# Key-length floor by a pairwise maximum on VectorE, and the division by the denominators on ScalarE, in the context attention of a decoder kernel

## The chip, the cores and the metric

The kernel runs on one core of a Trainium2 chip. A core has five engines that run their own instruction streams and meet at semaphores: TensorE (PE in the profile, with its weight loads as a row of their own, PEld), VectorE (DVE), ScalarE (ACT), GpSimd (POOL) and SyncE (SP), which only issues DMAs here. SBUF is the working memory and PSUM takes what TensorE writes. The metric is the device time of one execution in microseconds (us), as the median of several runs. Three runs of the kernel before gave 1176.01, 1176.21 and 1176.6 us.

## The reference, cut to what matters

The whole program is a two-layer decoder over x of shape (32, 56, 128): a state-space mixer, an attention over a context, a mixture of experts, and then the same three kinds once more, with a layer norm after each. Only the first layer's context attention is touched. Its inputs are the context (32, 1500, 128) with a mask, and x as 56 latents per batch. It has two heads of 64.

```
def rmsnorm(x, gamma):
    n = jnp.linalg.norm(x, axis=-1, keepdims=True) * x.shape[-1] ** (-0.5)
    return x / jnp.maximum(n, RMS_EPS) * gamma            # RMS_EPS = 1e-08
xn = layernorm(x, ln_x_g, ln_x_b)                         # x: the context here
ln = layernorm(latents, ln_l_g, ln_l_b)
q = ln @ W_q
kv = jnp.concatenate([xn @ W_kv, ln @ W_kv], axis=1)
...
qn = rmsnorm(q, q_gamma) * SCALE
kn = rmsnorm(k, k_gamma)
sim = jnp.einsum('bhid,bhjd->bhij', qn, kn)
sim = jnp.where(full_mask[:, None, None, :], sim, neg)
attn = jax.nn.softmax(sim, axis=-1)
out = jnp.einsum('bhij,bhjd->bhid', attn, v)
return out.transpose(0, 2, 1, 3).reshape(b, nl, INNER) @ W_out + b_out
```

## The kernel before

The stage in question is `stage_context` (lines 1184 to 1536). It treats the 32 batches one after the other in a pipeline. One batch's context of 1500 positions lies in SBUF as 125 partitions by 12 tiles of 128 features. The key matrix and the queries are folded together before the stage, so that a batch needs these products on TensorE: 12 transposes of the normalised context (`turn`, L1466), 12 products that give the keys whose lengths are needed (`keys`, L1483), 12 products that give raw scores with 12 for the mask before them (`scores`, L1494 and L1490), one transpose and one product that spread each column's maximum to all partitions (`turn_peaks` L1511, `widen_peaks` L1515), 12 products that mix the context by the probabilities (`mix`, L1531) and two that make the output rows with their denominators (`values`, L1522 and L1523). Data are f32, and each f32 product or weight load is two records in the trace.

Every engine runs the same loop: the function `steps` goes through 38 iterations k, and in each it calls the parts of that engine's list in the order written, a part with lag j working on batch k - j. This order is written by hand and is the whole schedule; each engine takes its instructions strictly in this order, with waits on semaphores.

- VectorE, in one iteration: `statistics` (12 bn_stats of batch k, L1302), `overall` (maximum of the transposed column maxima, L1341), `scale` (three multiplications of raw scores by the inverse key lengths, out of PSUM, L1314), `weigh` (batch k - 6), `maximum` (column maxima of the scores, L1334), `lengths` (batch k - 2). `weigh` waits for the output rows in PSUM, takes the reciprocal of the two denominators (L1322), waits for it, and multiplies the rows of each head by it (two instructions of 56 x 64, L1326) into `att`. `lengths` sums the squares of the keys in three reduces of 512 to 8 elements (L1348), waits for the third, and applies the floor 1e-16 * 64 to the 24 sums in place by a tensor_scalar (L1352).
- ScalarE: `evict_two` and `evict_last` (transposed context out of PSUM, L1364), `take_mix` (L1380), `inverse` (Ln and Exp of the floored sums, L1387 and L1389), `diagonal` (L1412), `exponential` (L1402 and L1405), `take_latents` (L1397), `square_two` and `square_last` (squares of the keys out of PSUM, L1426), `take_peak` (L1419), `normalise` (2 of the 12 tiles, L1439), `roots` (L1448, L1451). Their order is in the statement that ends the ScalarE block.
- GpSimd: `subtract` (the maxima from all 1456 scores of each partition, one long tensor_tensor, L1256), `normalise` (10 of the 12 tiles, L1266 to L1271), `moments` (six small operations, L1282 to L1290). At the start it fills eight buffers (L1251) and counts them in the semaphore `const`.
- SyncE loads a batch's context (750 KB) when its buffer is free (L1241).

TensorE's `mix` and `values` both write the PSUM bank `pO`, and both wait for `att` of the batch before, so the division must have read the rows of one batch before the next mix starts.

Of the kernel before, what the change touches and what calls it, by code (L numbers as in the profile page):

```python
# [16 lines left out]
ALU = mybir.AluOpType  # L17
# [7 lines left out]
P = 128  # L25
# [11 lines left out]
KP = 125  # L37
# [1146 lines left out]
def stage_context(core, sb, psum, mk, mv_ext, qw, latS, vl, att, bout, negmask, onehot, xc, ctx_loads):  # L1184
# [15 lines left out]
    shift = sb("shift", [KP, 2, KT])  # L1200
    xcT = sb("xcT", [D, 2, KT * KP])
    sq = sb("sq", [KP, 2, KS, HB, DH])
    ss = sb("ss", [KP, 2, KT, HB])
    inv = sb("inv", [KP, 2, KT, HB])
    sc = sb("sc", [P, 3, KT + 1, QR])
    top = sb("top", [P, 2, QR])
    topall = sb("topall", [P, 2, QR])
    plat = sb("plat", [P, QP])
    mixT = sb("mixT", [D, 2, QP])
    rden = sb("rden", [P, HB])  # L1210
    peak = sb("peak", [QR, 2])
    diag = sb("diag", [QR, 2, QR])
    pX = psum("pX", [P, SUB, 512])
# [6 lines left out]
             "top topT peak diag wide topall subbed probs mix mixT val rden att").split()  # L1220
    s = {n: core.sem(f"bl_{n}") for n in names}
    HALF = D // 2

    def context(n):
        return xc[:, n % NX] if n % NX < NX0 else more[:, n % NX - NX0]
# [8 lines left out]
    with nc.Block() as block:  # L1234
# [8 lines left out]
        @block.gpsimd  # L1243
        def _(pool):

            fills = [(sc[:, buf, KT, :], NEG) for buf in range(3)] + [(top[96:P, buf, :], NEG) for buf in range(2)]
            fills += [(plat[:, :], 0.0), (mixT[:, :, :], 0.0), (att[:, :, :], 0.0)]
            for m, (tile, value) in enumerate(fills):
                if m:
                    pool.wait_ge(s["const"], m)  # L1250
                pool.memset(tile, value).then_inc(s["const"], 1)  # L1251
            pool.wait_ge(s["const"], len(fills))

            def subtract(n):
                pool.wait_ge(s["topall"], n + 1)
                pool.tensor_tensor(sc[0:KP, n % 3, :, :], sc[0:KP, n % 3, :, :],  # L1256
                                   over(topall[0:KP, n % 2, :].unsqueeze(1), [KP, KT + 1, QR]),
                                   ALU.subtract).then_inc(s["subbed"], 1)

            def normalise(n):  # L1260
                b = n % 2
                pool.wait_ge(s["rstd"], n + 1)
                if n >= 2:
                    pool.wait_ge(s["xc_act"], n - 1)
                    pool.wait_ge(s["xc"], n - 1)
                pool.tensor_tensor(shift[:, b, :], total[:, b, :], rstd[:, b, :], ALU.mult).then_inc(s["shift"], 1)  # L1266
                pool.wait_ge(s["shift"], 2 * n + 1)
                pool.tensor_scalar(shift[:, b, :], shift[:, b, :], -0.5, 1.0, ALU.mult, ALU.add).then_inc(s["shift"], 1)
                pool.wait_ge(s["shift"], 2 * n + 2)
                for t in range(KT - KA):  # L1270
                    last = pool.tensor_scalar(context(n)[:, t, :], context(n)[:, t, :],  # L1271
                                              rstd[:, b, t:t + 1], shift[:, b, t:t + 1], ALU.mult, ALU.add)
                last.then_inc(s["xc"], 1)

            def moments(n):
                b = n % 2
                mean, sums = stats[:, b, :, 1::3], stats[:, b, :, 2::3]
                pool.wait_ge(s["stats"], n + 1)
                if n >= 2:
                    pool.wait_ge(s["shift"], 2 * n - 2)  # L1280
                    pool.wait_ge(s["lnv"], n - 1)
                pool.tensor_tensor(apart[:, b, :], mean[:, :, 0], mean[:, :, 1], ALU.subtract).then_inc(s["spread"], 1)  # L1282
                pool.tensor_tensor(total[:, b, :], mean[:, :, 0], mean[:, :, 1], ALU.add)
                pool.tensor_tensor(within[:, b, :], sums[:, :, 0], sums[:, :, 1], ALU.add).then_inc(s["spread"], 1)
                pool.wait_ge(s["spread"], 4 * n + 1)
                pool.tensor_tensor(apart[:, b, :], apart[:, b, :], apart[:, b, :], ALU.mult).then_inc(s["spread"], 1)
                pool.wait_ge(s["spread"], 4 * n + 3)
                pool.tensor_scalar(apart[:, b, :], apart[:, b, :], HALF / 2.0, None, ALU.mult).then_inc(s["spread"], 1)
                pool.wait_ge(s["spread"], 4 * n + 4)
                pool.tensor_tensor(within[:, b, :], within[:, b, :], apart[:, b, :], ALU.add).then_inc(s["within"], 1)  # L1290

            steps(((5, subtract), (1, normalise), (0, moments)))
            pool.tensor_tensor(core.x_tm[:, :, :], core.x_tm[:, :, :], over(bout[:, :].unsqueeze(1), [T2, NT, D]), ALU.add)

        @block.vector
        def _(ve):
# [8 lines left out]
            def scale(n):  # L1305
                ve.wait_ge(s["inv"], n + 1)
                if n >= 3:
                    ve.wait_ge(s["mix"], n - 2)
                if n == 0:
                    ve.wait_ge(s["const"], 8)  # L1310
                for u in range(SUB):
                    tiles = slice(u * KS, (u + 1) * KS)
                    ve.wait_ge(s["raw"], n * SUB + u + 1)
                    ve.tensor_tensor(sc[0:KP, n % 3, tiles, :].rearrange("p k (h q) -> p k h q", h=HB),  # L1314
                                     pS[0:KP, u, 0:KS * QR].rearrange("p (k h q) -> p k h q", k=KS, h=HB),
                                     over(inv[:, n % 2, tiles, :].unsqueeze(3), [KP, KS, HB, L]),
                                     ALU.mult).then_inc(s["scaled"], 1)

            def weigh(n):
                ve.wait_ge(s["val"], n + 1)  # L1320
                val = pO[:, val_at].rearrange("p (h v) -> p h v", v=VW)
                ve.reciprocal(rden[:, :], val[:, :, DH]).then_inc(s["rden"], 1)  # L1322
                ve.wait_ge(s["rden"], n + 1)
                for h in range(HB):
                    rows = slice(h * DH, h * DH + L)
                    last = ve.tensor_scalar(att[rows, n, :], val[rows, h, 0:DH], rden[rows, h:h + 1], None, ALU.mult)  # L1326
                last.then_inc(s["att"], 1)

            def maximum(n):
                ve.wait_ge(s["scaled"], SUB * (n + 1))  # L1330
# [12 lines left out]
            def lengths(n):  # L1343
                if n >= 2:
                    ve.wait_ge(s["lninv"], n - 1)
                for u in range(SUB):
                    ve.wait_ge(s["sq"], n * SUB + u + 1)
                    ve.tensor_reduce(ss[:, n % 2, u * KS:(u + 1) * KS, :], sq[:, (n * SUB + u) % 2, :, :, :], AX,  # L1348
                                     ALU.add).then_inc(s["ss"], 1)
                ve.wait_ge(s["ss"], SUB * (n + 1))  # L1350

                ve.tensor_scalar(ss[:, n % 2, :, :], ss[:, n % 2, :, :], 1e-16 * DH, None, ALU.max).then_inc(s["floor"], 1)  # L1352

            steps(((0, statistics), (4, overall), (3, scale), (6, weigh), (3, maximum), (2, lengths)))

        @block.scalar
        def _(act):
# [16 lines left out]
            def take_mix(n):  # L1374
                act.wait_ge(s["mix"], n + 1)
                if n >= 2:
                    act.wait_ge(s["val"], n - 1)
                if n == 0:
                    act.wait_ge(s["const"], 8)
                act.activation(mixT[:, n % 2, :].rearrange("p (h q) -> p h q", h=HB)[:, :, 0:L],  # L1380
                               pO[:, mix_at].rearrange("p (h q) -> p h q", h=HB), ACT.Copy).then_inc(s["mixT"], 1)

            def inverse(n):
                act.wait_ge(s["floor"], n + 1)
                if n >= 2:
                    act.wait_ge(s["scaled"], SUB * (n - 1))
                act.activation(inv[:, n % 2, :, :], ss[:, n % 2, :, :], ACT.Ln, scale=1.0 / DH).then_inc(s["lninv"], 1)  # L1387
                act.wait_ge(s["lninv"], n + 1)
                act.activation(inv[:, n % 2, :, :], inv[:, n % 2, :, :], ACT.Exp, scale=-0.5).then_inc(s["inv"], 1)  # L1389

            def take_latents(n):
# [1 line left out]
                    act.wait_ge(s["mix"], n - 2)  # L1393
                    act.wait_ge(s["probs"], 2 * (n - 2))
                if n == 0:
                    act.wait_ge(s["const"], 8)
                act.activation(sc[0:L, n % 3, KT, :].rearrange("p (h q) -> p h q", h=HB), latS[:, n, :, :],  # L1397
                               ACT.Copy).then_inc(s["lats"], 1)

# [33 lines left out]
            def square_last(n):  # L1433
                square(n, 2)

            def normalise(n):
                act.wait_ge(s["shift"], 2 * n + 2)
                for t in range(KT - KA, KT):
# [4 lines left out]
            def roots(n):  # L1443
                act.wait_ge(s["within"], n + 1)
                if n >= 2:
# [5 lines left out]
                act.activation(rstd[:, n % 2, :], rstd[:, n % 2, :], ACT.Exp, scale=-0.5).then_inc(s["rstd"], 1)  # L1451

            steps(((2, evict_two), (6, take_mix), (3, inverse), (2, evict_last), (4, diagonal), (5, exponential),
                   (3, take_latents), (2, square_two), (4, take_peak), (1, normalise), (2, square_last), (0, roots)))

        @block.tensor
        def _(pe):
# [47 lines left out]
            def turn_peaks(n):  # L1505
                pe.wait_ge(s["top"], n + 1)
                if n:
                    pe.wait_ge(s["topall"], n)
                if n == 0:
                    pe.wait_ge(s["const"], 8)  # L1510
                pe.transpose(pM[0:QR, topT_at], top[:, n % 2, :], core.ident[:, :]).then_inc(s["topT"], 1)  # L1511

            def widen_peaks(n):
# [1456 lines left out]
```

## Time and profile before

| | |
|---|---|
| median of three timed runs | 1176.21 us |
| span of the profiled execution | 1458.4 us |
| granted TensorE clock, mean of the span | 0.634 of full speed |
| busy: PE, PEld, DVE, ACT, POOL | 1326.6, 954.6, 995.0, 694.7, 608.6 us |
| the context stage in the span | from about 320 to 852 us, 32 batches |

The profile comes from one execution of its own. The page gives its span, 1458.4 us, as the time of that execution and no other figure for it; it is 282.2 us longer than the median of the timed runs. A row of the grouped view names the line, the engine, the operation, the tile written and the tiles read, the shapes, and the count, then the busy time and the idle time before these instructions with what ended it. Idle time is only of interest on the engine that sets the pace. The clock is given as a share of 2.4 GHz: 0.50 is 1.2 GHz and 1.00 is 2.4 GHz.

### The profile page before, as it was taken

To read this page: it belongs to the slowest core of one execution; us is meant where nothing else is said; L and a number is where in the kernel's file an instruction comes from. 1 tells how busy PE (TensorE), PEld (TensorE's weight loads), DVE (VectorE), ACT (ScalarE), POOL (GpSimd) and SP (SyncE) were. 2 spreads that over 40 slices of the span, in tenths; PEclk is the share of its full clock that TensorE was granted. 3 is DMA by queue.
4 is the path that set the end of the run, shared out by engine and by line. 5 is a ranking of instruction groups with operands and counts; after the bars stand their busy time and mean duration, and the time that the engine had idled before them with its cause. 6 is when DMAs were issued, how large, how long until landed. Compare 5 with 4: busy or idle time off the path is not lost. (4 is left out here: it accounts for less than half of the span.)

```text
span 1458.4 us, 22009 instructions
## 1 busy us (share of the span) xinstructions
PE 1326.6 (91%) x8207; PEld 954.6 (65%) x8207; DVE 995.0 (68%) x1835; ACT 694.7 (48%) x1465; POOL 608.6 (42%) x832
## 2 busy tenths in 40 slices
PE   8999997878999999999999999978298898889897
PEld 5555553647999999999999885742033333556736
DVE  6888699475777667767766534673988888567444
ACT  5655562344544444444444334445555555257442
POOL 6300000136755655655664222110488889314250
PEclk6566666666666666666666666666566666666666
DMA  3000000212111111111110001000100000000001
GB/s 63 1 1 2 1 1 1 69 55 87 40 46 43 54 54 43 48 59 44 44 43 1 1 1 20 1 1 0 56 1 0 1 0 1 1 1 3 2 0 26
DMA packets 18762, 33.34 MB, mean 23 GB/s; under 512 B 5200, under 2 KB 13888, under 8 KB 18656
## 3 DMA queue, kind: packets, MB, share of 16 engines
q1 hardware_dynamic: 18144, 31.89, 6.5%
q8 instruction: 65, 1.06, 0.3%
q14 instruction: 41, 0.34, 0.1%
q10 hardware_dynamic: 512, 0.05, 0.0%
HBM read 31.02 MB, written 0.92 MB: 22 GB/s over the span
## 5 line engine op out<-in xcount | busy, mean ns | idle before, releaser
L1256 POOL TENSOR_TENSOR bl_sc<-bl_sc,bl_topall 125x1456 f32<-125x1456 f32 x32 | 104.6, 3268 | 204.3 <-ACT bl_topall L1419 204.3
L2417 POOL TENSOR_TENSOR m_h_in<-m_dtu,xT 128x896 f32<-128x896 f32 x64 | 132.8, 2083 | 94.2 <-ACT xT L2438 93.9
L825 DVE SCALAR_TENSOR_TENSOR l0r_u<-l0r_u,l0r_a_col 128x1024 f32<-128x1024 f32 x110 | 136.1, 1277 | 17.8 <-ACT l0r_u L732 17.7
L1494 PE MATMUL bl_pS<-b_qw,bl_xcT 128*125 128x112 f32 x768 | 144.6, 336 | 0.0
L2494 DVE TENSOR_TENSOR_SCAN m_hs<-msp_da,m_h_in 128x896 f32<-128x896 f32 x64 | 129.1, 2019 | 6.6 <-ACT msp_da L2456 6.2
L732 ACT ACTIVATE l0r_u<-l0r_pu 128x512 f32<-128x512 f32 x218 | 112.0, 602 | 41.6 <-PE l0r_pu L632 41.4
L1483 PE MATMUL bl_pX<-b_mk,bl_xcT 128*125 128x128 f32 x768 | 131.5, 344 | 0.0
L1494 PEld LDWEIGHTS bl_pS<-b_qw,bl_xcT 128*125 128x125 f32 x768 | 130.9, 265 | 0.0
L1314 DVE TENSOR_TENSOR bl_sc<-bl_pS,bl_inv 125x448 f32<-125x448 f32 x96 | 59.5, 620 | 100.2 <-PE bl_pS L1494 100.2
L1483 PEld LDWEIGHTS bl_pX<-b_mk,bl_xcT 128*125 128x125 f32 x768 | 127.5, 254 | 0.2 <-ACT bl_xcT L1364 0.2
L632 PE MATMUL l0r_pu<-l0r_xs,l0r_eb 32*128 32x256 f32 x896 | 122.5, 556 | 3.5 <-ACT l0r_xs L716 2.2
L2376 PE MATMUL msp_py<-m_hc,ident 128*128 128x448 f32 x192 | 120.5, 772 | 2.6 <-DVE mg_gT L2485 2.6
L632 PEld LDWEIGHTS l0r_pu<-l0r_xs,l0r_eb 32*128 32x128 f32 x896 | 84.1, 238 | 40.7 <-ACT l0r_u L732 22.6
L1426 ACT ACTIVATE bl_sq<-bl_pX 125x512 f32<-125x512 f32 x96 | 56.9, 592 | 113.0 <-PE bl_pX L1483 112.7
L1364 ACT ACTIVATE bl_xcT<-bl_pX 128x500 f32<-128x500 f32 x96 | 56.0, 587 | 113.6 <-PE bl_pX L1466 112.1
L938 POOL MEMSET bq_lT<- 128x256 f32 x1 | 0.3, 312 | 217.8 <-POOLq L550 217.8
L1334 DVE TENSOR_REDUCE bl_top<-bl_sc 125x112 f32<-125x1456 f32 x32 | 85.3, 2664 | 1.0
L1348 DVE TENSOR_REDUCE bl_ss<-bl_sq 125x8 f32<-125x512 f32 x96 | 62.8, 682 | 26.9 <-ACT bl_sq L1426 26.7
L652 PE MATMUL l0r_py<-l0r_u,l0r_cexp 128*32 128x256 f32 x896 | 78.1, 525 | 0.0
L2456 ACT ACTIVATE msp_da<-m_dt,mw_alog 128x440 f32<-128x440 f32 x128 | 75.1, 624 | 0.1
L2438 ACT ACTIVATE xT<-msp_pb 128x448 f32<-128x448 f32 x64 | 34.7, 542 | 83.8 <-PE msp_pb L2353 83.8
L2376 PEld LDWEIGHTS msp_py<-m_hc,ident 128*128 128x128 f32 x192 | 43.0, 225 | 46.5 <-issue 44.3
(413 smaller groups left out, 2844.4 us busy)
## 6 DMA issues: line engine op xcount, KB each, us to landing
b_xc<-in_ctx SPq DMA_DIRECT2D x16, 750.0 KB
bl_more<-in_ctx SPq DMA_DIRECT2D x16, 750.0 KB
x_tm<-in_x SPq DMA_DIRECT2D x1, 896.0 KB, 8.5
cw_cT<-in_ctx_headT SPq DMA_DIRECT2D x1, 896.0 KB, 4.3
out_dram<-x_tm SPq DMA_DIRECT2D x4, 224.0 KB, 2.5
l0r_xr<-in_x SPq DMA_DIRECT2D x4, 192.0 KB, 4.7
w_up<-in_L_ffn_w SPq DMA_DIRECT2D x1, 512.0 KB, 4.1
w_down<-in_L_ffn_w SPq DMA_DIRECT2D x1, 512.0 KB, 5.3
```

The source lines that it names most:

```text
L632: last = pe.matmul(out, eb[rows, half, j0 + j, :, :], x, start=True, stop=True)
L652: last = pe.matmul(out, cexp[:, g, :], h, start=(c < half_way and j == 0), stop=(j == 3 and (c < half_way or half == 1)))
L732: act.activation(u[:, c % RC, :, :, at:at + 2 * B].rearrange("p t r x -> p (t r) x"), pu[:, n % NPU, :].rearrange("p (a x) -> p a x", x=2 ...
L825: ve.scalar_tensor_tensor(state(c, i, r), prev, a_col[:, :], state(c, i, r), ALU.mult, ALU.add).then_inc(s["step"], 1)
L1256: pool.tensor_tensor(sc[0:KP, n % 3, :, :], sc[0:KP, n % 3, :, :], over(topall[0:KP, n % 2, :].unsqueeze(1), [KP, KT + 1, QR]), ALU.subtra ...
L1334: ve.tensor_reduce(top[0:KP, n % 2, :], sc[0:KP, n % 3, :, :].rearrange("p k q -> p q k"), AX, ALU.max).then_inc(s["top"], 1)
L1483: last = pe.matmul(pX[0:KP, u, r * D:(r + 1) * D], xcT[:, n % 2, at], mk[:, :], start=True, stop=True)
L1494: last = pe.matmul(pS[0:KP, u, r * QR:(r + 1) * QR], xcT[:, n % 2, t * KP:(t + 1) * KP], qw[:, n, :], start=False, stop=(r == KS - 1))
L2376: last = pe.matmul(py[:, half, 0:CH], core.ident[:, :], of[:, half, :], start=(st == 0), stop=(st == DS - 1))
L2417: pool.tensor_tensor(h_in[:, n % NI, :, :], dtu[:, k % 2, :, :], both_halves(bs[:, n % NB, :]), ALU.mult).then_inc(s["db"], 1)
L2456: act.activation(da[:, n % 2, half * CH:(half + 1) * CH].rearrange("p (b t) -> p b t", t=L)[:, :, 1:L], dt[:, half, span(k)].rearrange("p ...
L2494: ve.tensor_tensor_scan(hs[:, n % NS, :, :].rearrange("p h q -> p (h q)"), da[:, n % 2, 0:H2 * CH], h_in[:, n % NI, :, :].rearrange("p h q ...
```

## The change

Two things are changed in `stage_context`.

The floor under the key lengths is no longer a tensor_scalar in place. The tile `ss` gets a last axis of two: slot 0 takes the sum of squares, slot 1 holds the constant floor, filled once by GpSimd as a ninth fill. A tensor_reduce with maximum over this pair writes a new tile `long`, which the logarithm reads. The wait for the fills moves from `scale` to the first `lengths`.

VectorE's `weigh` becomes `invert`, with the reciprocal alone, into one of two buffers. The two multiplications of 56 x 64 go to ScalarE as Copy activations with the reciprocal as scale, read out of PSUM, in a new part `weigh` between `take_latents` and `square_two`.

```diff
-    ss = sb("ss", [KP, 2, KT, HB])
+    ss = sb("ss", [KP, 2, KT, HB, 2])
+    long = sb("long", [KP, 2, KT, HB])
-    rden = sb("rden", [P, HB])
+    rden = sb("rden", [P, 2, HB])
+    FILLED = 9
 # gpsimd
-            fills += [(plat[:, :], 0.0), (mixT[:, :, :], 0.0), (att[:, :, :], 0.0)]
+            fills += [(plat[:, :], 0.0), (mixT[:, :, :], 0.0), (att[:, :, :], 0.0), (ss[:, :, :, :, 1], 1e-16 * DH)]
-            pool.wait_ge(s["const"], len(fills))
+            pool.wait_ge(s["const"], FILLED)
 # vector
-                if n == 0:
-                    ve.wait_ge(s["const"], 8)
...
-            def weigh(n):
+            def invert(n):
                 ve.wait_ge(s["val"], n + 1)
-                val = pO[:, val_at].rearrange("p (h v) -> p h v", v=VW)
-                ve.reciprocal(rden[:, :], val[:, :, DH]).then_inc(s["rden"], 1)
-                ve.wait_ge(s["rden"], n + 1)
-                for h in range(HB):
-                    rows = slice(h * DH, h * DH + L)
-                    last = ve.tensor_scalar(att[rows, n, :], val[rows, h, 0:DH], rden[rows, h:h + 1], None, ALU.mult)
-                last.then_inc(s["att"], 1)
+                if n >= 2:
+                    ve.wait_ge(s["att"], n - 1)
+                ve.reciprocal(rden[:, n % 2, :], pO[:, val_at].rearrange("p (h v) -> p h v", v=VW)[:, :, DH]).then_inc(s["rden"], 1)
...
-                    ve.tensor_reduce(ss[:, n % 2, u * KS:(u + 1) * KS, :], sq[:, (n * SUB + u) % 2, :, :, :], AX,
+                    ve.tensor_reduce(ss[:, n % 2, u * KS:(u + 1) * KS, :, 0], sq[:, (n * SUB + u) % 2, :, :, :], AX,
                                      ALU.add).then_inc(s["ss"], 1)
                 ve.wait_ge(s["ss"], SUB * (n + 1))
-
-                ve.tensor_scalar(ss[:, n % 2, :, :], ss[:, n % 2, :, :], 1e-16 * DH, None, ALU.max).then_inc(s["floor"], 1)
-
-            steps(((0, statistics), (4, overall), (3, scale), (6, weigh), (3, maximum), (2, lengths)))
+                if n == 0:
+                    ve.wait_ge(s["const"], FILLED)
+                ve.tensor_reduce(long[:, n % 2, :, :], ss[:, n % 2, :, :, :], AX, ALU.max).then_inc(s["floor"], 1)
+
+            steps(((0, statistics), (4, overall), (3, scale), (6, invert), (3, maximum), (2, lengths)))
 # scalar
-                act.activation(inv[:, n % 2, :, :], ss[:, n % 2, :, :], ACT.Ln, scale=1.0 / DH).then_inc(s["lninv"], 1)
+                act.activation(inv[:, n % 2, :, :], long[:, n % 2, :, :], ACT.Ln, scale=1.0 / DH).then_inc(s["lninv"], 1)
...
+            def weigh(n):
+                act.wait_ge(s["rden"], n + 1)
+                val = pO[:, val_at].rearrange("p (h v) -> p h v", v=VW)
+                for h in range(HB):
+                    rows = slice(h * DH, h * DH + L)
+                    last = act.activation(att[rows, n, :], val[rows, h, 0:DH], ACT.Copy, scale=rden[rows, n % 2, h:h + 1])
+                last.then_inc(s["att"], 1)
...
             steps(((2, evict_two), (6, take_mix), (3, inverse), (2, evict_last), (4, diagonal), (5, exponential),
-                   (3, take_latents), (2, square_two), (4, take_peak), (1, normalise), (2, square_last), (0, roots)))
+                   (3, take_latents), (6, weigh), (2, square_two), (4, take_peak), (1, normalise), (2, square_last), (0, roots)))
```

## Rows read from the trace of the kernel before

**Rows 1.** Busy by stretch: one period of the context stage; columns are named.

```profile
core 0: us, PE busy (x) PEld busy (x) DVE busy (x) ACT busy (x) POOL busy (x), PEclk, DMA share, GB/s
650.36:666.23 15.87, 15.87 (x105) 15.37 (x104) 10.96 (x26) 7.21 (x19) 9.15 (x20) 0.65 0.13 49
1000.00:1100.00 100.00, 66.18 (x127) 22.88 (x126) 75.11 (x52) 54.36 (x89) 51.32 (x25) 0.59 0.07 21
```

**Rows 2.** VectorE by line in the same period, idle time last.

```profile
L1348 DVE TENSOR_REDUCE bl_ss<-bl_sq 125x8 f32<-125x512 f32 x3 | 2.0, 681 | 0.5 <-ACT bl_sq L1426 0.5
L1314 DVE TENSOR_TENSOR bl_sc<-bl_pS,bl_inv 125x448 f32<-125x448 f32 x3 | 1.9, 621 | 3.3 <-PE bl_pS L1494 3.3
L1341 DVE TENSOR_REDUCE bl_peak<-bl_pM 112x1 f32<-112x128 f32 x1 | 0.3, 291 | 0.9 <-PE bl_pM L1511 0.9
```

**Rows 3.** Timeline, all engines, one period: start, length, what runs, idle before.

```profile
640.38 4.09 PE L1483 MATMUL bl_pX<-b_mk,bl_xcT 128*125 128x128 f32 x24
...
644.24 0.49 PE L1515 MATMUL bl_pM<-bl_diag,ones 112*128 112x112 f32 x2
...
644.57 4.04 PE L1531 MATMUL bl_pO<-bl_sc,b_xc 125*128 125x112 f32 x24
...
645.11 3.28 POOL L1256 TENSOR_TENSOR bl_sc<-bl_sc,bl_topall 125x1456 f32<-125x1456 f32 x1 [6.36 <-ACT bl_topall L1419]
...
646.32 0.69 DVE L1348 TENSOR_REDUCE bl_ss<-bl_sq 125x8 f32<-125x512 f32 x1 [0.55 <-ACT bl_sq L1426]
...
647.04 1.39 DVE L1352 TENSOR_SCALAR bl_ss<-bl_ss 125x24 f32<-125x24 f32 x1
...
654.50 0.28 ACT L1397 ACTIVATE bl_sc<-b_latS 56x112 f32<-56x112 f32 x1
...
656.25 4.09 PE L1483 MATMUL bl_pX<-b_mk,bl_xcT 128*125 128x128 f32 x24
656.46 0.62 DVE L1314 TENSOR_TENSOR bl_sc<-bl_pS,bl_inv 125x448 f32<-125x448 f32 x1 [0.97 <-PE bl_pS L1494]
657.00 0.16 DVE L1322 RECIPROCAL bl_rden<-bl_pO 128x2 f32<-128x2 f32 x1
657.19 0.58 DVE L1326 TENSOR_SCALAR bo_att<-bl_pO,bl_rden 56x64 f32<-56x64 f32 x2
657.74 0.60 ACT L1426 ACTIVATE bl_sq<-bl_pX 125x512 f32<-125x512 f32 x1 [2.96 <-PE bl_pX L1483]
657.80 2.66 DVE L1334 TENSOR_REDUCE bl_top<-bl_sc 125x112 f32<-125x1456 f32 x1
...
660.38 1.27 DVE L1348 TENSOR_REDUCE bl_ss<-bl_sq 125x8 f32<-125x512 f32 x2
660.44 4.04 PE L1531 MATMUL bl_pO<-bl_sc,b_xc 125*128 125x112 f32 x24
```

**Rows 4.** All instructions of L1352: durations min/median/max in ns.

```profile
L1352 DVE TENSOR_SCALAR bl_ss<-bl_ss x32: 177/1379/1782, 341.5 to 821.3; 125x24 f32<-125x24 f32 x32
```

**Rows 5.** VectorE by line, whole span: reduces of small shapes.

```profile
L1341 DVE TENSOR_REDUCE bl_peak<-bl_pM 112x1 f32<-112x128 f32 x32 | 9.3, 290 | 36.0 <-PE bl_pM L1511 36.0
L2696 DVE TENSOR_REDUCE cl_head<-cl_head 128x4 f32<-128x16 f32 x1 | 0.1, 113 | 0.0
```

**Rows 6.** ScalarE by line in the period of rows 1.

```profile
L1412 ACT ACTIVATE bl_diag<-ident,bl_peak 112x112 f32<-112x112 f32 x1 | 0.4, 378 | 0.0
L1380 ACT ACTIVATE bl_mixT<-bl_pO 128x112 f32<-128x112 f32 x1 | 0.3, 258 | 0.0
```

**Rows 7.** ScalarE's timeline at the end of the stage.

```profile
852.02 1.28 ACT L384 ACT_TABLE_LOAD   x1 [2.69 <-PEq L1234]
```

More of the change, by code:

```diff
@@ L1378, in take_mix @@
                 if n == 0:
-                    act.wait_ge(s["const"], 8)
+                    act.wait_ge(s["const"], FILLED)
                 act.activation(mixT[:, n % 2, :].rearrange("p (h q) -> p h q", h=HB)[:, :, 0:L],
@@ L1395, in take_latents @@
                 if n == 0:
-                    act.wait_ge(s["const"], 8)
+                    act.wait_ge(s["const"], FILLED)
                 act.activation(sc[0:L, n % 3, KT, :].rearrange("p (h q) -> p h q", h=HB), latS[:, n, :, :],
@@ L1509, in turn_peaks @@
                 if n == 0:
-                    pe.wait_ge(s["const"], 8)
+                    pe.wait_ge(s["const"], FILLED)
                 pe.transpose(pM[0:QR, topT_at], top[:, n % 2, :], core.ident[:, :]).then_inc(s["topT"], 1)
```

## The prediction

> **What bounds the kernel now.** I read the busy time by stretch first. In the context stage PE is busy for all of a 15.87 us period, at a granted clock of 0.65, which lies between the two levels of 1.2 and 2.4 GHz; DVE is busy for 10.96, POOL for 9.15 and ACT for 7.21 us [rows 1]. The timeline confirms the period: the keys product starts at 640.38 and again at 656.25, and the next groups of PE start before the one in front has drained (keys from 640.38 for 4.09 us, the widening at 644.24, the mix at 644.57) [rows 3]. VectorE by line comes next. Its idle time in the period is 0.5 + 3.3 + 0.9 = 4.7 us, and what ends it is PE or a square that itself had to wait for PE [rows 2]. So DVE is occupied for 15.87 - 4.7 = 11.2 us with the small gaps between its instructions. In the profiled execution PE sets the pace here, and no work taken from DVE can shorten the 32 periods.
>
> The timed runs are another matter. Their median is 1176.2 us against a span of 1458.4 us, 282.2 us less, and the instructions are the same. The likeliest reason is the clock. PE was busy for 1326.6 us in the profile. If the granted clock in a timed run is c, at most 1326.6 x (1 - 0.65/c) can be gained, so c must be at least 0.65/(1 - 282.2/1326.6) = 0.83. That is a floor: there are stretches, as 1000 to 1100 us, where PE is busy for only 66 us of 100 and DVE for 75 [rows 1], and there a faster PE gives less than its share. I take the timed clock to be near 1.00. PE then needs 15.87 x 0.65 = 10.3 us for a period, less than the 11.2 us that DVE is occupied. In the timed runs the two engines are therefore close rivals, and DVE's work may matter.
>
> **The change part by part.**
>
> The floor. The old tensor_scalar works on 24 elements and takes 177 ns at the least, but 1379 ns in the median and 1782 at the most [rows 4]. The timeline says what it does in between: it starts at 647.04 and ends at 648.43, and the long subtraction on POOL runs from 645.11 to 648.39 [rows 3]. It stands still until POOL is done, 0.04 us after it. The third length reduce ran at 646.32 beside the same subtraction and took 0.69 us, no more than the mean 0.68 of the three [rows 2, 3], so a reduce isn't held. The Trainium skill gives the mechanism (SBUF — State Buffer, section Who interferes with whom): a VectorE instruction in a two-port mode and GpSimd exclude each other for a whole instruction, one with a single SBUF input outside these modes does not contend. By this rule the new reduce is never held; the trace agrees in both rows, 1379 ns for the one kind and 0.69 us for the other.
>
> The new reduce takes 48 elements to 24. No row has this shape. From below, a reduce of 16 to 4 elements took 113 ns; from above, one of 128 to 1 out of PSUM took 290 [rows 5]. I take 0.20 us, about a third of the way, as 48 is nearer to 16. The saving is 1.38 - 0.20 = 1.2 us a period in the profile (1.09 to 1.27). If against the row above it were held as the old one is, the saving would be nothing. Slot 0 of `ss` is now written with a stride; 8 elements out of 512 read, I take nothing for it (bounds -0.1 to +0.1 us, a whole small reduce). ACT's logarithm reads a dense tile as before.
>
> In a timed run with a faster PE the old floor waits less. Counted from the moment when PE finishes the third group of scores: DVE's third scaling, reciprocal, division and maximum bring it to the length reduces after 660.38 - 656.46 = 3.92 us, and three of them with 0.65 between starts bring it to the floor at about 3.92 + 1.95 + 0.1 = 6.0 us. POOL's subtraction starts after keys (644.24 - 640.38 = 3.86 us, 2.5 at a clock of 1.00), widening and the copy of the maxima (0.9 us from 644.24 to 645.11, of which I leave 0.8), at 3.3, and ends at 6.6 [rows 3]. The floor would then take 0.6 to 0.7 us and not 1.38. DVE's path is 11.2 - 0.7 = 10.5, and with 0.1 us to notice the scores 10.6 us, against PE's 10.3.
>
> The division. DVE loses two instructions, 0.58 us, and the step to the next one: the maximum starts at 657.80, the division at 657.19, so 0.61 us a period [rows 3]. ACT gains two Copy activations of 64 elements with a pointer as scale. Out of PSUM without a pointer 112 elements took 258 ns, with a pointer out of SBUF 112 took 378 [rows 6]. I take 0.33 us each, nearer to the lower since 64 is less than 112 (bounds 0.25 and 0.38), 0.65 us for the pair. The Trainium skill speaks against the move (ScalarE: Activation LUTs, sections What ACT_TABLE_LOAD costs and Rules for kernel authors): multiplications belong on VectorE, and an ACTIVATE costs 186 ns plus 0.833 per element plus 93 for a pointer, an estimate of 332 ns for 64 elements. The trace has 284 ns for each of the old ones, half of 0.58 with the overlap, so by the page 0.66 us is paid for 0.58 us; as the two engines differ in load, this says nothing of the period.
>
> The wait that comes with it: ACT is in order, and its new part waits for DVE's reciprocal, which ends at 657.16, with the squares, the copy of the maxima, the normalisation and the last square queued behind it. ACT had been idle from 654.78 (654.50 + 0.28) to 657.74, so its time from 657.2 to 657.9 costs the first square 0.2 us [rows 3]. DVE takes the squares' sums only at 660.38, and the second square waited for PE in any case. PE's mix at 660.44 waits for `att`, which would be there at 657.9 and was at 657.77: 2.5 us to spare, and still 1.2 where PE is faster (keys and widening of 4.19 us shrink to 2.8, the division ends 1.6 after the scores). I cost the wait at nothing; without that cover it is 0.65 us a period at most. The new wait of `invert` for `att` two batches back is long met, and the reciprocal has two buffers.
>
> The edges. The ninth fill is at most a few tenths on POOL at the start, 19 us before the first floor at 341.5 [rows 4]; nothing. After the last batch ACT loads a table at 852.02 right behind the stage's end [rows 7]; the last division on ACT instead of DVE delays that by 0.1 to 0.2 us, once. Nothing else is issued, and no DMA moves.
>
> **The sum.** Against the profiled execution: 32 periods bound by PE at the clock of rows 1, 0, plus 0.2 at the end, 1458.4 to 1458.6 us of span. Against the timed runs, with a clock near 1.00: DVE's path falls from 10.6 by 0.5 for the floor and 0.6 for the division to 9.5, so PE takes over at 10.3, and each period is 0.3 us shorter. 32 x 0.3 = 9.6, less 0.2, is 9 us: 1176.2 - 9 = 1167 us. Its own range: if the floor is held for its full 1.38, DVE's path before is 11.3 and each period gives 1.0 us, 32 us in all, 1144; if the period is at PE's time already, 1176. So 1146 to 1174 for this case.
>
> **The rivals.** The first is no change: PE bounds the stage in the timed runs too. For it speaks every PE row of the profile and the floor of 0.83 on the clock, at which PE needs 12.4 us against DVE's 11.2; against it that this leaves no room for stretches not bound by PE. It gives 1176.2 + 0.2, 1176.4 us.
>
> The second is slower: the divisions on ACT sit in front of the squares, and the loop through ACT decides. Place: `weigh` in ACT's list. Price: where ACT is just in time, its 0.65 us move every square, and the copy of the maxima that starts POOL's subtraction; I take half, 0.3 us a period, 10 us, 1186 us, with 21 us at the most. It decides from the point where ACT comes to `square_two` after the first keys are in PSUM by more than the 2.5 us (1.2 with a fast PE) that PE's mix and the maximum leave. ACT's 7.21 + 0.65 = 7.9 us a period against 10.3 speaks against it; that the order is strict and the wait is on another engine speaks for it.
>
> A third is that DVE is in a closed chain with longer waits than I count, the timed period is well above 10.6, and all that is taken from DVE comes back: 1.8 us a period, 58 us, 1118 us. The room between 282 us and what the other stages can give allows it; that POOL, ACT and PE all have spare time against DVE's 11.2 bounds it at about 30 us. A fourth: the pair reduce is held as the scalar was. Then only the division's 0.6 counts, of which PE leaves 0.3: 1167 as well; it shows in the rows, not in the time.
>
> **How the numbers follow.** The forecast, faster by 9 us, has 0.50; the third rival, faster by 30 us or more, 0.06; no change 0.30; slower 0.14. A measurement of this kernel can tell about 0.2%, 2.4 us, from no change, and a little of the forecast's case lies within that. So faster 0.54, same 0.31, slower 0.15. For 8 in 10 the range reaches from 1146, the large end of the forecast's case, to 1181, half way into the slower one.
>
> **What would show it.** In the trace after, the reduce that writes `long` must take about 0.2 us while POOL's subtraction runs; the maximum must start 0.2 us after the reciprocal; two ACT instructions of about 0.33 us must stand between the latents and the squares; and the mix must not wait for `att`. PE rows without gaps and a period of 15.87 us at a clock of 0.65 would repeat the profile's bound. I am wrong if the time is within 2 us of before (PE bounds the timed runs), if the mix waits for ACT, or if the gain exceeds 32 us, which PE's 10.3 us forbid.

## The result and the profile after

The changed kernel is slower. Seven runs of it have a median of 1184.48 us (1178.35 to 1186.11), seven of the kernel before, on the same chip, 1176.14 us (1171.67 to 1176.6). The ratio is 1.0069, with an interval of 1.0045 to 1.0094: 8 us lost, where a gain of 9 was forecast.

The rows read for the prediction came from an execution whose granted clock was 0.634. The profile after comes from one at 0.910, with a span of 1179.5 us and a time of 1181.25. So the kernel before was profiled again: span 1169.5 us, time 1171.28, clock 0.928. "Before" is that second profile from here on, except where rows are named.

The first view is the busy time by stretch, well inside the stage; first the kernel before, then the one after.

```profile
core 0: us, PE busy (x) PEld busy (x) DVE busy (x) ACT busy (x) POOL busy (x), PEclk, DMA share, GB/s
400.00:500.00 100.00, 100.00 (x927) 97.83 (x927) 90.08 (x216) 66.97 (x163) 82.47 (x172) 1.00 0.19 70
...
480.51:491.65 11.14, 11.14 (x106) 10.90 (x104) 10.03 (x24) 7.35 (x19) 9.20 (x21) 1.00 0.19 70
```

```profile
core 0: us, PE busy (x) PEld busy (x) DVE busy (x) ACT busy (x) POOL busy (x), PEclk, DMA share, GB/s
400.00:500.00 100.00, 100.00 (x928) 97.80 (x927) 81.76 (x198) 71.74 (x180) 82.42 (x172) 1.00 0.19 71
...
483.40:494.54 11.14, 11.14 (x106) 10.90 (x104) 9.09 (x22) 8.07 (x20) 9.19 (x21) 1.00 0.19 72
```

The lower row of each is one period, from keys product to keys product, and answers to [rows 1]. At a clock of 1.00 it is 11.14 us in both, and PE has no gap in it. DVE is busy for 0.94 us less, ACT for 0.72 more, and the period doesn't move. VectorE by line in that period of the kernel after answers to [rows 2]:

```profile
L1344 DVE TENSOR_REDUCE bl_ss<-bl_sq 125x8 f32<-125x512 f32 x3 | 2.0, 684 | 0.1
L1314 DVE TENSOR_TENSOR bl_sc<-bl_pS,bl_inv 125x448 f32<-125x448 f32 x3 | 1.9, 623 | 1.9 <-PE bl_pS L1499 1.9
```

`scale` waits for 1.9 us there, and for 0.8 in the kernel before. Over the whole stage (320 to 680 us) its wait for PE grew from 26.7 to 52.8 us. The time freed on DVE became waiting on PE.

The two new operations are as small as expected. All instructions of their lines, in the kernel after (they answer to [rows 4] and [rows 6]); the third row is the old floor in the new profile of before:

```profile
L1349 DVE TENSOR_REDUCE bl_long<-bl_ss x32: 202/203/204, 306.3 to 644.9; 125x24 f32<-125x48 f32 x32
...
L1438 ACT ACTIVATE bo_att<-bl_pO,bl_rden x64: 295/309/310, 339.6 to 670.3; 56x64 f32<-56x64 f32 x64
```

```profile
L1352 DVE TENSOR_SCALAR bl_ss<-bl_ss x32: 178/427/449, 303.2 to 642.6; 125x24 f32<-125x24 f32 x32
```

So the loss is not in the 32 periods: from the first instruction of the stage (284.80 us before, 287.49 after) to the first mix that waits for a division it is 363.1 us before and 363.3 after. The timeline at the end of the stage has it: columns are start, length, engine, what runs, and in brackets the idle time before it with its releaser. First the kernel before:

```profile
647.88 2.90 PE L1531 MATMUL bl_pO<-bl_sc,bl_more 125*128 125x112 f32 x24 [1.28 <-DVE bo_att L1326]
...
652.08 0.17 DVE L1322 RECIPROCAL bl_rden<-bl_pO 128x2 f32<-128x2 f32 x1 [0.86 <-PE bl_pO L1523]
652.29 0.58 DVE L1326 TENSOR_SCALAR bo_att<-bl_pO,bl_rden 56x64 f32<-56x64 f32 x2
...
653.02 2.90 PE L1531 MATMUL bl_pO<-bl_sc,bl_more 125*128 125x112 f32 x24 [0.57 <-DVE bo_att L1326]
...
658.15 2.90 PE L1531 MATMUL bl_pO<-bl_sc,bl_more 125*128 125x112 f32 x24 [0.97 <-DVE bo_att L1326]
...
663.46 2.96 PE L2541 MATMUL f_ph<-ident,bo_att 128*64 128x128 f32 x16 [1.15 <-PEq L1234]
```

and the kernel after:

```profile
650.83 2.90 PE L1536 MATMUL bl_pO<-bl_sc,bl_more 125*128 125x112 f32 x24 [1.32 <-ACT bo_att L1438]
...
654.50 1.31 ACT L1399 ACTIVATE bl_sc<-bl_sc 125x1344 f32<-125x1344 f32 x1
655.03 0.17 DVE L1323 RECIPROCAL bl_rden<-bl_pO 128x2 f32<-128x2 f32 x1 [0.86 <-PE bl_pO L1528]
655.71 0.28 ACT L1402 ACTIVATE bl_plat<-bl_sc 56x112 f32<-56x112 f32 x1
655.90 0.62 ACT L1438 ACTIVATE bo_att<-bl_pO,bl_rden 56x64 f32<-56x64 f32 x2
...
656.66 4.53 PE L1536 MATMUL bl_pO<-bl_sc,bl_more 125*128 125x112 f32 x24 [1.26 <-ACT bo_att L1438]
...
663.96 4.53 PE L1536 MATMUL bl_pO<-bl_sc,bl_more 125*128 125x112 f32 x24 [1.51 <-ACT bo_att L1438]
...
670.89 1.28 ACT L384 ACT_TABLE_LOAD   x1 [0.27 <-PEq L1236]
670.93 3.54 PE L2546 MATMUL f_ph<-ident,bo_att 128*64 128x128 f32 x16 [1.18 <-PEq L1236]
```

In the last iterations of `steps` nothing new enters the pipeline. PE has little besides `mix` and `values`, and they form a closed chain with the division: values of batch n, reciprocal, division, mix of n + 1, `take_mix`, values of n + 1. On DVE the division starts 0.21 us after the reciprocal. On ACT it stands in order behind the exponential's two activations: the reciprocal is there from 655.20, the division starts at 655.90 and ends at 656.52. From the reciprocal's start to the division's end it is 0.79 us before and 1.49 after, and the mix waits 1.26 us instead of 0.57.

The second part of the loss is the length of a mix, 4.53 us against 2.90. The granted clock shows why. Between the first mix that waits and the first transposes behind the stage, before and after:

```profile
647.88:663.46 15.58, 11.95 (x88) 10.40 (x89) 5.08 (x11) 4.39 (x10) 10.13 (x3) 1.00 0.00 0
```

```profile
650.83:670.93 20.10, 15.20 (x87) 13.64 (x88) 2.62 (x5) 6.39 (x17) 11.02 (x3) 0.83 0.00 0
...
664.20:667.60 3.40, 3.40 (x18) 3.40 (x18) 0.00 (x0) 0.00 (x0) 0.42 (x1) 0.50 0.00 0
```

The clock is the last number but two of a row: 1.00 throughout before, 0.83 in the mean after, with parts of both last mixes at 0.50, which is 1.2 GHz. The 4.52 us between 15.58 and 20.10 are, but for 0.03, the waits, (1.26 - 0.57) + (1.51 - 0.97) = 1.23, and the mixes, 2 x (4.53 - 2.90) = 3.26. What PE did before the clock fell: it had waited 1.32 and 1.26 us, with a mix of 2.90 and short products between.

Right behind the drain the clock falls in the kernel before too (from 668 us on it is 1.00 again):

```profile
664.10:667.50 3.40, 3.40 (x19) 3.07 (x18) 1.53 (x4) 2.10 (x6) 0.00 (x0) 0.51 0.02 5
```

What the change adds is that it falls inside the drain, during the mixes.

### The profile page after: what moved, and what is told of

Its sections match the earlier page's. It is cut to its first block and busy times, and to the rows that moved or that the text cites. A ratio compares the mean times of both kernels' runs of the same rounds, so it can differ in the third digit from the quotient of the medians.

```text
span 1179.5 us, 22041 instructions
## 1 busy us (share of the span) xinstructions
PE 992.9 (84%) x8207; PEld 741.2 (63%) x8207; DVE 942.2 (80%) x1771; ACT 706.5 (60%) x1529; POOL 610.2 (52%) x833
## 5 line engine op out<-in xcount | busy, mean ns | idle before, releaser
L632 PE MATMUL l0r_pu<-l0r_xs,l0r_eb 32*128 32x256 f32 x896 | 107.3, 458 | 6.0 <-ACT l0r_u L732 3.9
L1499 PE MATMUL bl_pS<-b_qw,bl_xcT 128*125 128x112 f32 x768 | 104.0, 278 | 0.0
L632 PEld LDWEIGHTS l0r_pu<-l0r_xs,l0r_eb 32*128 32x128 f32 x896 | 73.7, 208 | 38.6 <-ACT l0r_u L732 28.0
L2381 PE MATMUL msp_py<-m_hc,ident 128*128 128x448 f32 x192 | 94.2, 622 | 3.2 <-DVE mg_gT L2490 3.2
L1499 PEld LDWEIGHTS bl_pS<-b_qw,bl_xcT 128*125 128x125 f32 x768 | 91.5, 189 | 0.0
L1488 PE MATMUL bl_pX<-b_mk,bl_xcT 128*125 128x128 f32 x768 | 90.2, 274 | 0.0
L1488 PEld LDWEIGHTS bl_pX<-b_mk,bl_xcT 128*125 128x125 f32 x768 | 87.0, 189 | 0.2 <-ACT bl_xcT L1361 0.2
L830 DVE TENSOR_SCALAR l0r_u<-l0r_u 128x1024 f32<-128x1024 f32 x112 | 72.2, 688 | 0.0
L1273 POOL TENSOR_SCALAR bl_more<-bl_more,bl_rstd,bl_shift 125x128 f32<-125x128 f32 x160 | 69.5, 457 | 1.7
L1273 POOL TENSOR_SCALAR b_xc<-b_xc,bl_rstd,bl_shift 125x128 f32<-125x128 f32 x160 | 69.5, 457 | 1.7
```

The lines of the kernel that those rows point to most:

```text
L632: last = pe.matmul(out, eb[rows, half, j0 + j, :, :], x, start=True, stop=True)
L1488: last = pe.matmul(pX[0:KP, u, r * D:(r + 1) * D], xcT[:, n % 2, at], mk[:, :], start=True, stop=True)
L1499: last = pe.matmul(pS[0:KP, u, r * QR:(r + 1) * QR], xcT[:, n % 2, t * KP:(t + 1) * KP], qw[:, n, :], start=False, stop=(r == KS - 1))
L2381: last = pe.matmul(py[:, half, 0:CH], core.ident[:, :], of[:, half, :], start=(st == 0), stop=(st == DS - 1))
```

## The experiments

All kernels below ran beside the kernel before; ratios are to it. "Drain" is the stretch just defined, from the first mix that waits to the first transposes of the next stage. The expectations measure it from the start of the last column maximum to the first copy out of those transposes; that is 16.98 us before and 22.43 after (some 0.7 of it because the maximum no longer stands behind the division), and is given as the long drain. Filler products and spare activations, where there are any, write what nothing reads.

**Both kernels once more.** Nothing is edited. The expectation of the first names two theories of the periods, A and B.

> The kernel before, unchanged, to have its trace at the clock of the timed runs and the size of a null difference. Every theory: 1176 us, ratio 1.000 within 0.2%. Theory A (PE bounds the steady periods of the context stage in both kernels): period 11.1 us as in the trace of the changed kernel, with no PE idle time. Theory B (the changed kernel's periods are longer because the divisions sit in front of the squares): period 10.8 to 10.9 us, 0.25 us shorter than in the changed kernel.

> The changed kernel, unchanged, beside the others on one chip. Every theory: 1184 us, ratio 1.007.

Measured: before 1174.75 us, 0.9982 [0.9957, 1.0007]; after 1183.13 us, 1.0068 [1.0043, 1.0093]. The drain of the second profile of after is 20.10 us again, with the same three waits to 0.01 us (long drain 22.42). The loss is no accident of one profile. The period of 11.14 us in both kernels is what theory A says; theory B wanted 10.8 to 10.9 before.

**Each part alone.** One kernel has the pairwise floor and the old division, the other the old floor and the division on ACT:

```
-            steps(((0, statistics), (4, overall), (3, scale), (6, invert), (3, maximum), (2, lengths)))
+            steps(((0, statistics), (4, overall), (3, scale), (6, weigh), (3, maximum), (2, lengths)))
...
```

```
-                ve.tensor_reduce(long[:, n % 2, :, :], ss[:, n % 2, :, :, :], AX, ALU.max).then_inc(s["floor"], 1)
+                ve.tensor_scalar(ss[:, n % 2, :, :], ss[:, n % 2, :, :], 1e-16 * DH, None, ALU.max).then_inc(s["floor"], 1)
...
```

> Only the floor by the pairwise reduce; VectorE keeps the division. Theory A or B with the division as the cause: 1174 to 1176 us, ratio 0.998 to 1.000. Theory C (the loss comes with the floor: the ninth fill, the strided sums, the shifted wait or the placement of the tiles behind the larger ss): 1184 us, ratio 1.007.

> Only the division moved to ScalarE; the floor stays a tensor_scalar. Theories with the division as the cause: 1184 us, ratio 1.007. Theory C: 1176 us, ratio 1.000.

Measured: floor alone 1175.49 us, 0.9996 [0.9976, 1.0017], drain 15.57 (long 17.06); division alone 1182.02 us, 1.005 [1.003, 1.0069], drain 20.10 (long 22.43). The floor is worth nothing, and the division alone loses as much as the whole change within the intervals, with the same drain.

**Where the division's loss sits.** The last four batches' divisions go back to DVE, or only these go to ACT (`n < B - 4` in the first line); ScalarE's `weigh` returns at once for the batches that DVE divides:

```
+                if n >= B - 4:
+                    ve.wait_ge(s["rden"], n + 1)
+                    for h in range(HB):
+                        rows = slice(h * DH, h * DH + L)
+                        last = ve.tensor_scalar(att[rows, n, :], val[rows, h, 0:DH], rden[rows, n % 2, h:h + 1], None, ALU.mult)
+                    last.then_inc(s["att"], 1)
```

> The changed kernel, but the last four of the 32 divisions stay on VectorE (the other 28 on ScalarE). Theory D (the loss is made in the four last iterations, where the engines are empty and ScalarE's exponential stands in front of the division on the only chain): all of the loss goes, 1175 to 1177 us, ratio 0.998 to 1.002; from the start of the last column maximum to the first transposed output 17.0 us as before, not 22.4. Theory E (the loss is made by the divisions in the 28 full iterations, or by the longer ScalarE program): 1182 to 1184 us, ratio 1.006.

> The opposite: only the last four divisions are on ScalarE, 28 stay on VectorE; the floor is the pairwise reduce. Theory D: the loss is whole, 1182 to 1184 us, ratio 1.005 to 1.007, the end of the stage 22.4 us. Theory E: 1176 to 1177 us, ratio 1.001.

Measured: last four on DVE 1176.58 us, 1.0006 [0.9991, 1.0022]; only the last four on ACT 1181.69 us, 1.0054 [1.0032, 1.0076]. Their long drains are 16.76 and 23.94 us. The drains as rows, in that order:

```profile
651.61:667.19 15.58, 11.94 (x87) 10.40 (x88) 5.10 (x11) 4.38 (x10) 10.11 (x3) 1.00 0.00 0
```

```profile
648.06:669.68 21.62, 16.72 (x87) 14.87 (x88) 2.61 (x5) 6.38 (x17) 11.01 (x3) 0.71 0.00 0
```

The divisions of four batches out of 32, moved to ACT, make the kernel slower; those of the other 28 cost nothing that can be measured. With the same three waits as in the kernel after, 1.32, 1.26 and 1.51 us, the last mix took 5.43 us here and not 4.53: what the clock costs varies with when it falls.

**Work on ACT without the wait.** The kernel before, with two spare activations of the same shape in each iteration of ACT's list:

```
+            def idle(n):
+                if n >= 2:
+                    act.wait_ge(s["rest"], n - 1)
+                for h in range(HB):
+                    rows = slice(h * DH, h * DH + L)
+                    last = act.activation(spare[rows, n % 2, :], core.ident[rows, 0:DH], ACT.Copy, scale=core.ident[rows, 0:1])
+                last.then_inc(s["rest"], 1)
...
```

> The kernel before, with two more Copy activations of 56 x 64 with a pointer as scale in every iteration on ScalarE, at the place where the changed kernel divides; they read a constant tile and nobody waits for them, so only their time and their place in the program are added. Theory D: 1175 to 1177 us, ratio 1.000 to 1.002 (they can hold the copy of the last maxima by 0.3 us, once or twice). Theory E: 1182 us or more, ratio 1.005.

Measured: 1179.66 us, 1.0023 [1.0001, 1.0044], drain 16.13 with a clock of 1.00 (long 17.38). The first two waits are those of before, 1.28 and 0.57, but the third is longer and has another releaser:

```profile
661.92 1.26 PE L1540 MATMUL bl_pO<-bl_sc,bl_more 125*128 125x112 f32 x9 [1.49 <-ACT bl_sc L1403]
```

ACT's order again: the spare pair delays `take_peak`, with it POOL's subtraction and the exponential, and the mix waits for the probabilities. Work on ACT that nothing waits for isn't free in the drain either, but it costs 0.55 us of drain and not 4.5. The time was a miss for both theories: 2.7 us by the ratio, where D had 0 to 2 and E 6. The interval of the ratio reaches from 0.1 to 5.2 us, so it doesn't tell 2.7 from the 0.55; what the rest of it is, if it is there, stays open.

**The clock by itself.** The kernel after, with filler products of 128 x 128 on PE in the gaps: one ahead of each of the last three `values` and four ahead of the last three mixes:

```
+            def fill(count):
+                for _ in range(count):
+                    pe.matmul(pX[:, 0, 0:P], core.ident[:, :], core.ident[:, :], start=True, stop=True)
...
             def values(n):
+                if n >= B - 3:
+                    fill(1)
...
             def mix(n):
+                if n == B - 3:
+                    pe.wait_ge(s["sq"], SUB * B)
+                if n >= B - 3:
+                    fill(4)
```

They write the bank of the keys, so the first four wait until the last squares have been taken from it.

> The changed kernel with extra products on TensorE in the last three iterations, 128 x 128 of a constant into a free bank: four ahead of each of the last three mixes and one ahead of each of their values, less than the gaps there (1.3 and 0.35 us), so that TensorE has less idle time while the chain is the same. Theory F (most of what the end of the stage loses is TensorE's clock, which fell to 1.2 GHz after its waits for the division had grown from 0.6 and 1.0 to 1.3 and 1.5 us): the last mixes take 2.9 us and not 4.5, the end of the stage is 18 to 19.5 us, the time 1178 to 1180. Without the clock (only the waits count): the end stays at 22.4 us and the time at 1183.

Measured: 1176.36 us, 1.0003 [0.9984, 1.0022], long drain 19.06: the rows are those of theory F, the time is 1.6 us below its 1178 to 1180. The drain and the last mix:

```profile
651.02:668.15 17.13, 14.63 (x109) 12.96 (x110) 2.63 (x5) 6.38 (x17) 11.03 (x3) 1.00 0.00 1
...
662.81 2.90 PE L1546 MATMUL bl_pO<-bl_sc,bl_more 125*128 125x112 f32 x24 [0.71 <-ACT bo_att L1438]
```

The releaser is still ACT, and from the last product of `values` to the second mix it takes 2.15 us, against 2.16 without the fillers; only PE has something to do meanwhile. The clock stays at 1.00 and every mix takes 2.90 us. The 1.55 us over the 15.58 of before are the waits behind ACT (1.23) and 0.3 for which the exponential ahead of the last mix waits for POOL's subtraction, a wait that the slow mix had hidden. The Trainium skill (TensorE: Matmul & The Clock Gate, section HAM oscillation — how this bites in real kernels) says that bursts of products with waits between them let the clock fall, so that the next burst starts cold. The runs agree: 4.53 us with the gaps, 2.90 with the same gaps filled. In the page's example the waits are longer than the bursts, though; here 1.32 and 1.26 us around a mix of 2.90 were enough.

**The same fillers without the change, and beside the last four on DVE.** In the second kernel two fillers, not four, stand ahead of a mix.

> The kernel before with the extra products alone (four ahead of each of the last three mixes, one ahead of the values). VectorE divides within 0.6 to 1.0 us there, so four products of 0.22 us in the gaps can cost up to 0.3 us in one of them. Theory F gives nothing to gain in the stage's end, as its clock was full already: 1175 to 1177 us, ratio 0.999 to 1.001. A gain of 3 us or more would say that the extra products help by something other than the clock in the changed kernel's last mixes.

> The candidate that might beat both: 28 divisions on ScalarE, the last four on VectorE, the pairwise floor, and extra products of a constant in TensorE's gaps of the last three iterations (two ahead of each mix, one ahead of the values). The end of the stage stays at 17 us, as no clock fell there without them; if TensorE's clock behind the stage gains from them, 1173 to 1175 us, if not 1176, ratio 0.997 to 1.001.

Measured: before with fillers 1176.56 us, 1.0001 [0.9978, 1.0025]; the last four on DVE with fillers 1177.51 us, 1.0013 [0.9991, 1.0034], so the hoped-for gain isn't there. Where the clock stays up anyway fillers bring nothing; they repair the change and don't beat the kernel before.

**A better place on ACT.** The last four divisions stand between the long activation of the exponential and the short one:

```
-                   (3, take_latents), (6, weigh), (2, square_two), (4, take_peak), (1, normalise), (2, square_last), (0, roots)))
+                   (6, late_weigh), (5, exponential_latents), (3, take_latents), (6, early_weigh), (2, square_two), (4, take_peak), (1, normalise), (2, square_last), (0, roots)))
```

> The changed kernel with ScalarE's order changed for the last four batches alone: the division stands between the long exponential (on which the next mix waits) and the short one of the latents, no longer behind the short one. By the chain at the end of the stage two waits of TensorE shrink by the 0.2 to 0.3 us of the short exponential, to 1.0 and 1.2 us. If what counts is how long TensorE waits before the last mixes, they run at 2.4 GHz again (2.9 us) and the end of the stage is 18 to 19 us, the time 1177 to 1179. If only engine time counts, the end is 21.9 us, the time 1182.

Measured: 1183.48 us, 1.0067 [1.0043, 1.009], long drain 23.05: nothing is repaired, a miss. The last two mixes and the clock from the second to behind the third:

```profile
658.89 5.43 PE L1546 MATMUL bl_pO<-bl_sc,bl_more 125*128 125x112 f32 x24 [1.35 <-ACT bo_att L1440]
...
667.23 5.33 PE L1546 MATMUL bl_pO<-bl_sc,bl_more 125*128 125x112 f32 x24 [1.02 <-ACT bo_att L1440]
```

```profile
658.70:672.30 13.60, 12.03 (x52) 11.30 (x52) 0.17 (x1) 3.00 (x8) 7.73 (x2) 0.50 0.00 0
```

The third wait is 0.5 us shorter, the second is not, and the clock fell ahead of the second mix and stayed at 0.50 for both. The new place also did more than it was meant to. The division now stands in front of `take_latents`, and DVE's last column maximum waits for that copy, which ends at 653.10; PE's transposition of the maxima waits for it in turn:

```profile
653.18 2.70 DVE L1330 TENSOR_REDUCE bl_top<-bl_sc 125x112 f32<-125x1456 f32 x1 [1.39 <-issue]
...
655.94 0.32 PE L1526 MATMUL bl_pM<-ident,bl_top 128*112 128x128 f32 x1 [0.43 <-DVE bl_top L1330]
```

So PE idled for 0.43 + 1.35 = 1.78 us around the second `values`, against 0.24 + 1.26 = 1.50 in the kernel after. This kernel doesn't tell what shorter waits would do, only that this order doesn't give them. That the second wait brings the clock down, and not the third, fits the kernel with spare activations: waits of 1.28, 0.57 and 1.49 us, and a clock of 1.00 through its drain.

## Why the prediction was wrong

**The clock of the timed runs.** Right in its direction: 1.00 in the periods of the stage, 0.91 to 0.93 over the span, above the floor of 0.83.

**PE's period, the term that was mis-sized.** It is why the forecast gain did not come. The prediction scaled 15.87 us by 0.65 to 10.3. Measured is 11.14. Not all of PE's time follows the clock: the keys product went from 4.09 us [rows 3] to 2.80 and the mix from 4.04 to 2.84, factors of 0.68 and 0.70, and 15.87 x 0.70 is 11.1. DVE was busy for 10.03 us of the period before and waited for others for 1.0, so its path was 11.14 - 1.0 = 10.1. The prediction had 10.6. So DVE was close, as said, but on the wrong side of PE by a microsecond, and the forecast gain of 0.3 us a period was nil. The first rival, no change, had the right mechanism for the 32 periods. (The range that the prediction gives its own case, 1146 to 1174, is 2 us narrower at both ends than the 1144 and 1176 that it works out; nothing hangs on it.)

**The floor.** The new price was right: the pair reduce took 203 ns (0.20 said) with 2 ns of spread under POOL's subtraction. The old one took 427 ns at full clock, held for less than the 0.6 to 0.7 expected. The rule of the Trainium skill (SBUF — State Buffer, section Who interferes with whom), by which a reduce is not held, agrees with this. The floor is worth nothing, as the kernel with the floor alone shows.

**The division.** 309 ns each, 0.63 us for the pair (0.65 said). In the period the mix started 1.28 us after it (486.25 against 484.97), with 1.2 forecast: the step "the mix must not wait for `att`" held wherever the pipeline is full. The rule of the Trainium skill (ScalarE: Activation LUTs, section Rules for kernel authors), that multiplications belong on VectorE, points the right way, but for another reason: the 0.63 against 0.58 us of the pair is not where the time went.

**The edges: the step that failed.** It is why the kernel became slower. The prediction charged the end of the stage once with 0.1 to 0.2 us for the last division, and costed the wait of the mix for `att` at nothing. The last division itself costs no more than that: the transposes behind it wait 1.18 us and not 1.15. But the prediction didn't ask what the last iterations look like, where no other work covers the chain through the division. There the same order costs 0.04, 0.69 and 0.54 us in three waits, and then PE's clock, 3.26 us. The mix waits for ACT, one of the signs of being wrong that the prediction named. The trace of before would have told. This row of its waits over the stage (us in total, times, longest) has TensorE's mix behind the division on DVE, twice, both at the end of the stage:

```profile
PE bl_pO L1531 <- DVE bo_att L1326: 2.2, 2, 1.2
```

The prediction uses this wait nowhere. The slower rival had the right engine and the right cause, ACT's strict order, but put it at the squares in 32 periods; that its 1186 us came near the result is luck.

**What the sum is now.** Between the two profiles lie 10.0 us. 2.7 of them are there at the first instruction of the stage, in front of everything that was changed; kernels that tie with before began up to 6 us later too, so this is the difference between executions. From that instruction to the end it is 884.8 us before and 892.0 after, 7.3 more before rounding: 0.3 up to the first mix that waits, 4.5 in the drain, 2.5 behind the first transposes. The ratio says 8 in the median. The drain's part is shown: it goes when the four divisions go back, and most of it when the clock is kept up.

The 2.5 goes with PE's clock. From the first transposes to the end, before and after, PE runs the same number of instructions and is busy for 4.9 us more:

```profile
663.46:1169.50 506.04, 383.94 (x2690) 233.46 (x2690) 399.43 (x697) 285.81 (x549) 262.97 (x151) 0.90 0.03 8
```

```profile
670.93:1179.50 508.57, 388.88 (x2690) 235.80 (x2690) 399.06 (x697) 286.28 (x549) 262.39 (x151) 0.89 0.03 8
```

Over all profiles that stretch is the longer, the longer PE is busy in it: 383.8 to 383.9 us with 505.4 to 506.1 in four kernels, 384.7 to 387.4 with 506.7 to 507.6 in five, and 388.6 to 388.9 with 508.5 to 508.7 in the three profiles with every division on ACT in the old place and no fillers. What moves the clock there is not settled. It isn't the slow drain alone: the two other kernels that have one are at 506.7 and 506.8, and the tying kernel with the last four on DVE at 507.0. From the stage's first instruction to the end, the kernels that tie with before need 884.2 to 885.8 us (888.0 with the fillers beside the divisions on ACT), the one with spare activations 885.9, and those with the last divisions on ACT and no fillers 891.6 to 892.5. So the profile shows 4.0 us brought back by the fillers, and the ratios some 7.7; the intervals of the two ratios leave room for both.

## What to carry to other kernels

Read the last iterations of a software pipeline as a stage of their own: there an instruction moved to another engine stands in its order with nothing to cover it. Ask the list of waits for the tile that the change touches, over the whole stage and not one period: the wait that mattered here was there only twice, both times in the drain. And ask what else stands behind the part that is moved, as the column maximum stood behind `take_latents`. When scaling a period to another clock, take two instruction groups seen at both clocks, not the mean clock.

## What the runs showed of the hardware

A difference of 0.7 us in one wait of TensorE, with 0.5 in the next, came with 3.3 us in two mixes. Where the drain began with waits of 1.32 and 1.26 us or more and no fillers, the clock fell from 1.00 to 0.50 inside it, in all five profiles; where it began with 1.28 and 0.57 it did not, in all four (0.56 in one). With the gaps of 1.32 and 1.26 us partly filled by products that nothing reads, it stayed at 1.00 (one profile).

The profile that the prediction was made from stood at a clock of 0.65 in its context stage, in each of eight neighbouring stretches of 2 us (600 to 616 us), so this was no change between long stretches at 0.50 and at 1.00. The period of f32 products is less sensitive to the clock than its share says: 0.65 against 1.00 made 15.87 us into 11.14, a factor of 0.70. Moving the divisions of 28 batches, 0.6 us each, from an engine busy for 90% of the stage to one at 67% changed nothing measurable (1.0006, up to 1.0022).
